# A four-layer graph kernel on one core: the opening's row blocks pass in three groups (0, 1-3, 4-7) instead of two halves

## The chip, the core and the metric

One NeuronCore of a Trainium2 chip. The metric is device time in microseconds (us) of one execution; lower is better. Matrices are float32.

## The reference, cut to what matters

x is 4096 x 128, adj is 4096 x 4096 (about one entry in a thousand, and the diagonal, are not zero). Four graph layers follow one another, each on h = relu(layernorm(x)), each added to x. Only the first touches the change:

```python
h = jnp.maximum(_layernorm(x, axis=-1), 0.0)
x = x + _L0_gnn_ref(L0_gnn_t, h, adj, L0_gnn_alpha, L0_gnn_W, L0_gnn_b)

def _L0_gnn_ref(t, x, A, alpha, W, b):
    a = alpha[0]
    A_prime = a * A
    diag = jnp.diagonal(A_prime) + (1.0 - a)
    A_prime = A_prime.at[jnp.arange(N), jnp.arange(N)].set(diag)
    out_degree = A_prime.sum(axis=1)
    inv_deg = jnp.where(out_degree == 0.0, 0.0, 1.0 / out_degree)
    x = inv_deg[:, None] * A_prime @ x
    x = x @ W.T + b
    return jax.nn.relu(x)
```

The later layers are two-head graph attention (1), one-head graph attention (2), both masked by adj > 0, and a product with adj turned, divided by column sums (3).

## The kernel before, in words

The 4096 rows are 32 row blocks of 128 (T = 32), in four quarters of S = 8 blocks. X keeps all row blocks in on-chip memory, G keeps for each row block what the product with the adjacency reads: here relu(layernorm(x)) times the turned weight W0, which the code calls projected. Stage 0 computes acc = adj x G, one quarter of the result rows at a time: `run(0, q, hooks)` on TensorE goes over k = 0 to 31, and for each k multiplies the adjacency tile k (128 x 1024, 512 KB, from in_adj_t) with G's row block k: eight products of 128 x 129 columns, L488, each of which appears in the trace as two records. A hook is a step that TensorE runs after a certain k. SyncE (SP) issues the loads of x and of the tiles in one order on one queue; eight slots hold tiles, so tile k + 8 is issued when TensorE has read tile k (slot_used) and VectorE has masked it (mask_made, L1361, which writes adj > 0 as bytes for the later layers).

Before k = 0 the row blocks 0 to 7 must be normalised and projected. This opening does it thus. SP loads blocks 0-3 (256 KB, x_first), 4-7 (256 KB, x_loaded[0]), then W0 (64 KB, w0_loaded), adjacency tiles 0 and 1, blocks 8-15, tiles 2 to 7, blocks 16-23. TensorE runs seven warm-up products (L628, WARM = 7), turns the eight blocks (L633) into two banks of PSUM, one for each half, waits for ScalarE's copy of each half to U (L819), multiplies with a centring matrix (identity less 1/128, L638), which subtracts the mean, waits for ScalarE's relu of each half into V (L822), and projects each half by W0 (L645). VectorE meanwhile takes the statistics of the eight blocks (L1127, L1131), combines them to the variance (L1134 to L1140), and after ScalarE's square root (L800) takes the reciprocal (L1146). ScalarE scales blocks 0-3 into G (L830), VectorE blocks 4-7 (L1347). In the same program order VectorE then begins its masks, one for each tile, and between them, after masks 0, 1 and 2, does the statistics of blocks 8-15 and their scale and shift (L1127 to L1150). ScalarE normalises these (L788) into V, and TensorE turns them (L519) in the hook of k = 5, and projects them (L542) in the hook of k = 6; blocks 16-23 follow in the hooks of k = 12 and 14, blocks 24-31 in those of 18 and 21. run(0, 0) waits for G's row block k at each k below 5, and at k = 8, 16 and 24.

Each engine executes its instructions in program order, and waits are on semaphores: an engine that waits holds up all that stands behind on it.

Of the kernel before, what the change touches and what calls it, by code (L numbers as in the profile page):

```python
# [30 lines left out]
P = 128  # L31
ALU = mybir.AluOpType
# [4 lines left out]
EPS = 1e-5  # L37
# [27 lines left out]
def graph_layers(nc, x, adj, adj_t, diag, alpha, w0_t, bias0, ff0, ff0_t, ff1_t, attn, g1, b1, g2, b2,  # L65
                 w2, w2_t, a2, out, inputs1):
    N, D = x.shape
# [19 lines left out]
    WARM = 7  # L87

    with ExitStack() as ctx:
# [73 lines left out]
        one = mix[:, 2, 0:P]  # L163
        U2 = U[:, 0:QC].rearrange("p (c i) -> p c i", c=2)
# [173 lines left out]
        def _(sp):  # L338
# [42 lines left out]
            load_x(0, S // 2, x_first)  # L381
            load_x(S // 2, S // 2, x_loaded[0])
# [96 lines left out]
        def _(pe):  # L479
# [147 lines left out]
            for i in range(WARM):  # L627
                pe.matmul(one, V[:, 0, :], V[:, 0, :], start=True, stop=True, skip_group_check=True)  # L628
            pe.wait_ge(consts_made, 2)
            for half in range(2):  # L630
                pe.wait_ge(x_loaded[0] if half else x_first, 16)
                for s in range(half * HALF, (half + 1) * HALF):
                    mm = pe.transpose(turn[:, s * P:(s + 1) * P], X[:, s, :], ident[:, :])  # L633
                mm.then_inc(f_turned if half else h_turned, 1)
            pe.wait_ge(centre_made, 1)
            for half in range(2):
                pe.wait_ge(xt_kept, half + 1)
                pe.matmul(turn[:, half * BANK:(half + 1) * BANK], centre, U[:, half * BANK:(half + 1) * BANK],  # L638
                          start=True, stop=True, skip_group_check=True).then_inc(x_centred, 1)
            pe.wait_ge(w0_loaded, 16)  # L640
            own = [feed(0, p, w0T, D, 0, 0) for p in range(Q)]
            for half in range(2):
                pe.wait_ge(f_wide if half else h_wide, 1)
                for s in range(half * HALF, (half + 1) * HALF):
                    mm = pe.matmul(mixed[:, s * P:(s + 1) * P], V[:, s, :], w0T, start=True, stop=True, skip_group_check=True)  # L645
                mm.then_inc(f_projected if half else h_projected, 1)
# [8 lines left out]
            run(0, 0, {5: own[1][0], 6: own[1][1], 12: own[2][0], 14: own[2][1], 18: own[3][0], 21: own[3][1],  # L655
# [121 lines left out]
        def _(act):  # L777
# [37 lines left out]
            def first_rows():  # L815

                for half in range(2):
                    act.wait_ge(f_turned if half else h_turned, 1)
                    act.copy(U[:, half * BANK:(half + 1) * BANK], turn[:, half * BANK:(half + 1) * BANK]).then_inc(xt_kept, 1)  # L819
                for half in range(2):  # L820
                    act.wait_ge(x_centred, half + 1)
                    act.activation(V[:, half * HALF:(half + 1) * HALF, :], turn[:, half * BANK:(half + 1) * BANK]  # L822
                                   .rearrange("p (s d) -> p s d", d=D), ACT.Relu).then_inc(f_wide if half else h_wide, 1)
                    if half == 0:
                        deviation(f_var, 1, f_dev)
                act.wait_ge(h_projected, 1)
                act.wait_ge(f_scale, 1)
                settle()
                for s in range(HALF):
                    act.activation(G[:, 0, s, 0:D], mixed3[:, s, :], ACT.Copy, scale=scale[:, s:s + 1])\  # L830
                        .then_inc(h_placed if s < HALF - 1 else f_norm, 1)

            def feed(h, p, q, between=()):
# [17 lines left out]
                else:  # L851
                    deviation(f_var, p - Q + 1 if h > 2 else p + 1, f_dev)
                    act.wait_ge(f_scale, p - Q + 1 if h > 2 else p + 1)
# [259 lines left out]
        def _(dve):  # L1113
# [8 lines left out]

            def statistics(src, made):

                def half():
                    for s in range(S // 2):
                        dve.bn_stats(stats[:, s, :], src(s))  # L1127

                def rest():
                    for s in range(S // 2, S):  # L1130
                        ins = dve.bn_stats(stats[:, s, :], src(s))  # L1131
                    st.then(ins)

                    dve.tensor_tensor(twice, stats[:, :, 1], stats[:, :, 4], ALU.add)  # L1134
                    dve.tensor_tensor(apart, stats[:, :, 1], stats[:, :, 4], ALU.subtract)
                    st.then(dve.tensor_tensor(squares, stats[:, :, 2], stats[:, :, 5], ALU.add))
                    dve.tensor_scalar(mean[:, :], twice, 0.5, None, ALU.mult)
                    dve.tensor_tensor(apart, apart, apart, ALU.mult)
                    st.then(dve.tensor_scalar(squares, squares, 1.0 / D, EPS, ALU.mult, ALU.add))
                    dve.scalar_tensor_tensor(var[:, :], apart, 0.25, squares, ALU.mult, ALU.add).then_inc(made, 1)  # L1140
                return [half, rest]
# [14 lines left out]
            def feed(h, p, q):  # L1156

                c = p - Q + 1 if h > 2 else p + 1
# [172 lines left out]
            dve.memset(V[:, 0, :], 0.0).then_inc(nothing_made, 1)  # L1331
# [4 lines left out]
            own = [feed(0, p, p) for p in range(Q)]  # L1336
# [3 lines left out]
            own[0][0]()  # L1340
            dve.wait_ge(x_loaded[0], 16)
            own[0][1]()
            own[0][2]()

            dve.wait_ge(f_scale, 1)
# [343 lines left out]
```

## Time and profile before

| | us |
|---|---|
| median of three runs | 1197.39 |
| lowest, highest | 1197.26, 1198.12 |
| span of the profiled execution | 1195.6 |
| PE (TensorE matmul) busy | 1190.9 |
| DVE (VectorE) busy | 939.5 |
| ACT (ScalarE) busy | 301.6 |

The span runs from the first to the last instruction of one profiled execution; the runs' times hold what lies around it too. A timeline row gives the start, the time from there to the end of the last of its instructions, the engine, line, operation, what is written from what, their count, and in brackets the idle time of the engine before it and what ended that. Matmul records overlap: the step from one start to the next is shorter than the duration of one.

### The profile page before, as it was taken

How to read it: one execution, taken by the hardware profiler on the slowest of the kernel's cores; microseconds unless marked ns; L12 is line 12 of the kernel's file. 1: busy time of each engine (PE TensorE's matmuls, PEld its weight loads, DVE VectorE, ACT ScalarE, POOL GpSimd, SP SyncE). 2: the span in 40 equal slices, each digit the busy share in tenths (PEclk: the TensorE clock that was granted, in tenths of full speed). 3: DMA queues.
4: the chain of work that ended last, by engine and by line, in shares of the span. 5: the costliest groups of instructions: out<-in, count | busy, mean ns of one | idle time of the engine just before them, and what ended most of it. 6: DMA issues, size and time to landing. Idle time of an engine off the chain costs nothing.

```text
span 1195.6 us, 16808 instructions
## 1 busy us (share of the span) xinstructions
PE 1190.9 (100%) x6299; PEld 823.9 (69%) x6299; DVE 939.5 (79%) x1704; ACT 301.6 (25%) x732; POOL 10.0 (1%) x21
## 2 busy tenths in 40 slices
PE   9999999999999999999999999999999999999999
PEld 9999999965444444444554547999999974444455
DVE  5448675798978787889788797798787869886886
ACT  3312122235323242422333144541212121000000
POOL 3000000000000000000000000000000000000000
PEclk9999999999999999999999999999999999999999
DMA  9888888700111102110000000022303068999830
GB/s 324 295 269 293 295 292 302 254 25 8 46 18 36 18 35 35 53 18 18 1 18 0 18 1 19 2 90 106 141 0 141 1 261 305 310 334 319 320 86 18
DMA packets 79284, 153.18 MB, mean 128 GB/s; under 512 B 35456, under 2 KB 44016, under 8 KB 79216
## 3 DMA queue, kind: packets, MB, share of 16 engines
q1 hardware_dynamic: 53264, 145.43, 34.8%
q10 hardware_dynamic: 25456, 6.30, 2.4%
q8 instruction: 43, 0.70, 0.2%
q0 software_dynamic: 496, 0.55, 0.2%
q14 instruction: 25, 0.20, 0.1%
HBM read 144.33 MB, written 4.24 MB: 124 GB/s over the span
## 4 chain that ended last, share of the span: by engine, by line
PE 98%; DVE 1%; ACT 0%; issue 0%; DVEq 0%
PE acc L504 51%; PE acc L488 37%; PE acc L761 4%; PE mix L570 1%; PE mix L557 1%; PE mix L542 1%; PE turn L519 1%; PE acc L769 1%; DVE ring L1323 0%; PE turn L515 0%; PE mix L628 0%; ACT V L788 0%; DVE U L1454 0%; PE turn L638 0%; PE mix L645 0%
## 5 line engine op out<-in xcount | busy, mean ns | idle before, releaser
L1323 DVE SCALAR_TENSOR_TENSOR ring<-G,score,mask 128x1024 f32<-128x1024 f32 x372 | 467.0, 1280 | 76.5 <-PE acc L504 42.9
L504 PE MATMUL acc<-ring,G 128*128 128x512 f32 x1000 | 436.2, 593 | 0.2 <-DVE acc L1263 0.2
L504 PEld LDWEIGHTS acc<-ring,G 128*128 128x128 f32 x1000 | 186.7, 190 | 227.0 <-issue 213.4
L488 PE MATMUL acc<-G,ring 128*128 128x129 f32 x2240 | 253.8, 275 | 0.0
L488 PEld LDWEIGHTS acc<-G,ring 128*128 128x128 f32 x2240 | 252.0, 192 | 0.8 <-issue 0.8
L488 PE MATMUL acc<-G,mask 128*128 128x129 f32 x1648 | 186.2, 275 | 0.0
L488 PEld LDWEIGHTS acc<-G,mask 128*128 128x128 f32 x1648 | 185.0, 192 | 0.0
L504 PE MATMUL acc<-mask,G 128*128 128x512 f32 x384 | 165.8, 593 | 0.0
L1597 DVE TENSOR_TENSOR ring<-ring,mask 128x1024 f32<-128x1024 f32 x120 | 146.8, 1223 | 10.7
L504 PEld LDWEIGHTS acc<-mask,G 128*128 128x128 f32 x384 | 72.6, 190 | 90.9 <-issue 89.7
L1361 DVE TENSOR_SCALAR mask<-mask 128x1024 uint8<-128x1024 f32 x103 | 68.5, 689 | 38.0 <-DMA mask<-in_adj_t 37.6
L800 ACT ACTIVATE dev<-var 128x8 f32<-128x8 f32 x28 | 5.9, 209 | 230.9 <-DVE var L1140 230.9
L978 ACT COPY U<-acc 128x512 f32<-128x512 f32 x22 | 12.9, 586 | 171.6 <-PE acc L504 171.6
L761 PE MATMUL acc<-mask,G 128*128 128x384 f32 (+1 forms) x128 | 48.6, 540 | 0.0
L986 ACT COPY U<-acc 128x387 f32<-128x387 f32 (+1 forms) x24 | 10.4, 446 | 129.7 <-PE acc L488 128.9
L761 PEld LDWEIGHTS acc<-mask,G 128*128 128x128 f32 x128 | 24.2, 190 | 24.0 <-issue 15.6
L788 ACT ACTIVATE V<-X,shift,scale 128x128 f32<-128x128 f32 (+1 forms) x88 | 35.0, 481 | 0.0
L784 ACT ACT_TABLE_LOAD x26 | 33.4, 1283 | 2.7 <-ACT V L788 1.6
L780 ACT COPY cols<-ident 128x1 f32<-128x1 f32 x40 | 7.6, 190 | 83.0 <-DVE V L1177 23.4
L788 ACT ACTIVATE V<-U,shift,scale 128x128 f32<-128x128 f32 x64 | 25.5, 481 | 6.4 <-DVE shift L1150 6.4
L1177 DVE SCALAR_TENSOR_TENSOR V<-G,ring 128x128 f32<-128x128 f32 x96 | 21.3, 288 | 5.3 <-ACT G L788 5.2
L788 ACT ACTIVATE U<-U,inv 128x128 f32<-128x128 f32 x64 | 19.5, 388 | 0.0
(210 smaller groups left out, 692.9 us busy)
## 6 DMA issues: line engine op xcount, KB each, us to landing
mask<-in_adj SPq DMA_DIRECT2D x128, 512.0 KB, 5.5
mask<-in_adj_t SPq DMA_DIRECT2D x103, 512.0 KB, 4.9
ring<-in_adj_t SPq DMA_DIRECT2D x18, 512.0 KB, 5.0
G<-given_rows SPq DMA_DIRECT2D x10, 512.0 KB, 3.9
G<-in_adj_t SPq DMA_DIRECT2D x4, 512.0 KB, 5.3
inputs<-V ACTq DMA_DIRECT2D x4, 512.0 KB, 2.7
V<-inputs SPq DMA_DIRECT2D x4, 512.0 KB, 3.9
X<-in_x SPq DMA_DIRECT2D x3, 512.0 KB, 8.6
```

The costliest lines, as they stand in the source:

```text
L488: mm = pe.matmul(acc[:, b, (s % 3) * DW:(s % 3) * DW + DW], lhs[:, s * P:(s + 1) * P], g, start=(k == 0 and s % 3 == 0), stop=(k == T - 1) ...
L504: mm = pe.matmul(acc[:, c, :], g, moving[:, c * BANK:(c + 1) * BANK], start=(k == 0), stop=(k == T - 1), skip_group_check=True)
L519: mm = pe.transpose(turn[:, s * P:(s + 1) * P], V[:, s, :], ident[:, :])
L542: mm = pe.matmul(dst, U[:, s * P:(s + 1) * P], weights, start=True, stop=True, skip_group_check=True)
L761: mm = pe.matmul(acc[:, c, 0:n], G[:, 0, k, 0:P], stream3[:, k, c * BANK:c * BANK + n], start=(k == 0), stop=(k == T - 1), skip_group_chec ...
L784: act.activation(warm[func], ident[:, 0:1], func)
L788: ins = act.activation(dst(s), src(s), func, bias=add(s), scale=mul(s))
L978: act.copy(U2[:, c, :], acc2[:, c, :]).then_inc(acc_taken, 1)
L1177: ins = dve.scalar_tensor_tensor(V[:, s, :], blocks(G[:, 1, :, :], q, 1, s)[:, 0, 0:D], 1.0, dot_w[c], ALU.mult, ALU.mult, accum_out=block ...
L1323: dve.scalar_tensor_tensor(slots[k % L], late_home[h] if early and k >= EARLY else rows_home[h, q], rank[h][:, k:k + 1], span(mask, (q * T ...
L1361: dve.tensor_scalar(span(mask, (q * T + k) * QC, QC), tile0(q, k), 0.0, None, ALU.is_gt).then_inc(mask_made, 1)
L1597: dve.tensor_tensor(added, stream3[:, 0, :] if k == 1 else added, stream3[:, k, :], ALU.add).then_inc(tile_added, 1)
```

## The change

The eight row blocks of the opening go in three groups of one, three and four blocks. Block 0 is loaded alone (64 KB), blocks 1-7 in one load (448 KB). Group 0 is turned and centred in bank 0 of `turn` and projected into `one` (bank 2 of `mix`), group 1 in bank 1 of `turn` and in bank 0 of `mix`, group 2 in bank 0 of `turn` again and in bank 1 of `mix`. TensorE's warm-ups become four ahead and two single ones between steps, into bank 2 of `acc`. On TensorE the order is: turn 0, centre 0, turn 1, wait for W0, project 0, turn 2, centre 1, project 1, then k = 0, centre 2, k = 1, project 2, k = 2. VectorE takes block 0's statistics and scale by themselves, then those of blocks 1-7; after that it waits, as before, for the projection of blocks 4-7 and scales them into G, ahead of its first mask. ScalarE copies, rectifies, takes two square roots and scales in the order of the groups. The counts that later steps wait for on f_var and f_scale are one higher.

```diff
--- before.py
+++ after.py
@@ -84,7 +84,8 @@
     EB = len(EDGE)
     SPARE = 2
     WEIGHTS = 15
-    WARM = 7
+    WARM = 4
+    STARTS = (slice(0, 1), slice(1, S // 2), slice(S // 2, S))
 
     with ExitStack() as ctx:
         def sb(name, shape, dt=F32):
@@ -161,6 +162,8 @@
         mixed = mix[:, 0:2, :].rearrange("p b c -> p (b c)")
         mixed3 = mixed.rearrange("p (s d) -> p s d", d=D)
         one = mix[:, 2, 0:P]
+        turned_x = (turn[:, 0:P], turn[:, BANK:BANK + (HALF - 1) * P], turn[:, 0:HALF * P])
+        projected_x = [one if s == 0 else mixed[:, s * P:(s + 1) * P] for s in range(S)]
         U2 = U[:, 0:QC].rearrange("p (c i) -> p c i", c=2)
         acc2 = acc[:, 0:2, :]
 
@@ -378,8 +381,8 @@
                         sp.wait_ge(tile_added, (q - 1) * (T - 1) + max(k, 1))
                     sp.dma_start(stream3[:, k, :], span(adj[k * P:(k + 1) * P, :], q * QC, QC)).then_inc(deep_loaded[k], 16)
 
-            load_x(0, S // 2, x_first)
-            load_x(S // 2, S // 2, x_loaded[0])
+            load_x(0, 1, x_first)
+            load_x(1, S - 1, x_loaded[0])
             sp.dma_start(w0T, w0_t).then_inc(w0_loaded, 16)
             layer0(0, range(2))
             load_x(S, S, x_loaded[1])
@@ -624,26 +627,40 @@
 
 
             pe.wait_ge(nothing_made, 1)
-            for i in range(WARM):
-                pe.matmul(one, V[:, 0, :], V[:, 0, :], start=True, stop=True, skip_group_check=True)
+            def warm_up(n):
+                for i in range(n):
+                    pe.matmul(acc[:, NB - 1, 0:P], V[:, S - 1, :], V[:, S - 1, :], start=True, stop=True, skip_group_check=True)
+
+            def turn_x(g):
+                pe.wait_ge(x_loaded[0] if g else x_first, 16)
+                for i, s in enumerate(range(S)[STARTS[g]]):
+                    mm = pe.transpose(turned_x[g][:, i * P:(i + 1) * P], X[:, s, :], ident[:, :])
+                mm.then_inc(h_turned if g < 2 else f_turned, 1)
+
+            def centre_x(g):
+                pe.wait_ge(xt_kept, g + 1)
+                some = slice(STARTS[g].start * P, STARTS[g].stop * P)
+                pe.matmul(turned_x[g], centre, U[:, some], start=True, stop=True, skip_group_check=True).then_inc(x_centred, 1)
+
+            def project_x(g):
+                pe.wait_ge(h_wide if g < 2 else f_wide, g + 1 if g < 2 else 1)
+                for s in range(S)[STARTS[g]]:
+                    mm = pe.matmul(projected_x[s], V[:, s, :], w0T, start=True, stop=True, skip_group_check=True)
+                mm.then_inc(h_projected if g < 2 else f_projected, 1)
+            warm_up(WARM)
             pe.wait_ge(consts_made, 2)
-            for half in range(2):
-                pe.wait_ge(x_loaded[0] if half else x_first, 16)
-                for s in range(half * HALF, (half + 1) * HALF):
-                    mm = pe.transpose(turn[:, s * P:(s + 1) * P], X[:, s, :], ident[:, :])
-                mm.then_inc(f_turned if half else h_turned, 1)
+            turn_x(0)
+            warm_up(1)
             pe.wait_ge(centre_made, 1)
-            for half in range(2):
-                pe.wait_ge(xt_kept, half + 1)
-                pe.matmul(turn[:, half * BANK:(half + 1) * BANK], centre, U[:, half * BANK:(half + 1) * BANK],
-                          start=True, stop=True, skip_group_check=True).then_inc(x_centred, 1)
+            centre_x(0)
+            turn_x(1)
             pe.wait_ge(w0_loaded, 16)
+            project_x(0)
+            turn_x(2)
+            centre_x(1)
+            warm_up(1)
+            project_x(1)
             own = [feed(0, p, w0T, D, 0, 0) for p in range(Q)]
-            for half in range(2):
-                pe.wait_ge(f_wide if half else h_wide, 1)
-                for s in range(half * HALF, (half + 1) * HALF):
-                    mm = pe.matmul(mixed[:, s * P:(s + 1) * P], V[:, s, :], w0T, start=True, stop=True, skip_group_check=True)
-                mm.then_inc(f_projected if half else h_projected, 1)
 
             def scores_behind_projections():
                 pe.wait_ge(weights_loaded, 16 * WEIGHTS)
@@ -652,7 +669,7 @@
                     mm = pe.matmul(one[:, 2 * h:2 * h + 2], raw, attnc[:, 2 * h:2 * h + 2], start=True, stop=True,
                                    skip_group_check=True)
                 mm.then_inc(qv_summed, 1)
-            run(0, 0, {5: own[1][0], 6: own[1][1], 12: own[2][0], 14: own[2][1], 18: own[3][0], 21: own[3][1],
+            run(0, 0, {0: lambda: centre_x(2), 1: lambda: project_x(2), 5: own[1][0], 6: own[1][1], 12: own[2][0], 14: own[2][1], 18: own[3][0], 21: own[3][1],
                        28: scores_behind_projections})
 
             def turn_weights_back():
@@ -814,21 +831,37 @@
 
             def first_rows():
 
-                for half in range(2):
-                    act.wait_ge(f_turned if half else h_turned, 1)
-                    act.copy(U[:, half * BANK:(half + 1) * BANK], turn[:, half * BANK:(half + 1) * BANK]).then_inc(xt_kept, 1)
-                for half in range(2):
-                    act.wait_ge(x_centred, half + 1)
-                    act.activation(V[:, half * HALF:(half + 1) * HALF, :], turn[:, half * BANK:(half + 1) * BANK]
-                                   .rearrange("p (s d) -> p s d", d=D), ACT.Relu).then_inc(f_wide if half else h_wide, 1)
-                    if half == 0:
-                        deviation(f_var, 1, f_dev)
-                act.wait_ge(h_projected, 1)
-                act.wait_ge(f_scale, 1)
-                settle()
-                for s in range(HALF):
-                    act.activation(G[:, 0, s, 0:D], mixed3[:, s, :], ACT.Copy, scale=scale[:, s:s + 1])\
-                        .then_inc(h_placed if s < HALF - 1 else f_norm, 1)
+                def columns(g):
+                    return slice(STARTS[g].start * P, STARTS[g].stop * P)
+
+                def keep_turned_x(g):
+                    act.wait_ge(h_turned if g < 2 else f_turned, g + 1 if g < 2 else 1)
+                    act.copy(U[:, columns(g)], turned_x[g]).then_inc(xt_kept, 1)
+
+                def keep_centred_x(g):
+                    act.wait_ge(x_centred, g + 1)
+                    act.activation(V[:, STARTS[g], :], turned_x[g].rearrange("p (s d) -> p s d", d=D), ACT.Relu)\
+                        .then_inc(h_wide if g < 2 else f_wide, 1)
+
+                def place(g):
+                    act.wait_ge(h_projected, g + 1)
+                    act.wait_ge(f_scale, 2 if g else 1)
+                    settle()
+                    for s in range(S)[STARTS[g]]:
+                        act.activation(G[:, 0, s, 0:D], projected_x[s], ACT.Copy, scale=scale[:, s:s + 1])\
+                            .then_inc(h_placed if s < HALF - 1 else f_norm, 1)
+                keep_turned_x(0)
+                keep_centred_x(0)
+                act.wait_ge(f_var, 1)
+                act.activation(dev[:, 0:1], var[:, 0:1], ACT.Sqrt).then_inc(f_dev, 1)
+                keep_turned_x(1)
+                place(0)
+                keep_centred_x(1)
+                act.wait_ge(f_var, 2)
+                act.activation(dev[:, 1:], var[:, 1:], ACT.Sqrt).then_inc(f_dev, 1)
+                keep_turned_x(2)
+                place(1)
+                keep_centred_x(2)
 
             def feed(h, p, q, between=()):
 
@@ -849,8 +882,8 @@
                     first_rows()
                     return
                 else:
-                    deviation(f_var, p - Q + 1 if h > 2 else p + 1, f_dev)
-                    act.wait_ge(f_scale, p - Q + 1 if h > 2 else p + 1)
+                    deviation(f_var, p - Q + 2 if h > 2 else p + 2, f_dev)
+                    act.wait_ge(f_scale, p - Q + 2 if h > 2 else p + 2)
                     settle()
                     if h == 4:
                         normalise(lambda s: blocks(G[:, 0, :, :], q, 1, s)[:, 0, 0:D], of_x, local(scale), local(shift),
@@ -1120,6 +1153,18 @@
             def wide(t):
                 return t[:, :].unsqueeze(2).broadcast_to([P, S, D])
 
+            def moments(made, some=slice(0, S)):
+
+                def of(t):
+                    return t[:, some]
+                dve.tensor_tensor(of(twice), stats[:, some, 1], stats[:, some, 4], ALU.add)
+                dve.tensor_tensor(of(apart), stats[:, some, 1], stats[:, some, 4], ALU.subtract)
+                st.then(dve.tensor_tensor(of(squares), stats[:, some, 2], stats[:, some, 5], ALU.add))
+                dve.tensor_scalar(of(mean), of(twice), 0.5, None, ALU.mult)
+                dve.tensor_tensor(of(apart), of(apart), of(apart), ALU.mult)
+                st.then(dve.tensor_scalar(of(squares), of(squares), 1.0 / D, EPS, ALU.mult, ALU.add))
+                dve.scalar_tensor_tensor(of(var), of(apart), 0.25, of(squares), ALU.mult, ALU.add).then_inc(made, 1)
+
             def statistics(src, made):
 
                 def half():
@@ -1130,14 +1175,7 @@
                     for s in range(S // 2, S):
                         ins = dve.bn_stats(stats[:, s, :], src(s))
                     st.then(ins)
-
-                    dve.tensor_tensor(twice, stats[:, :, 1], stats[:, :, 4], ALU.add)
-                    dve.tensor_tensor(apart, stats[:, :, 1], stats[:, :, 4], ALU.subtract)
-                    st.then(dve.tensor_tensor(squares, stats[:, :, 2], stats[:, :, 5], ALU.add))
-                    dve.tensor_scalar(mean[:, :], twice, 0.5, None, ALU.mult)
-                    dve.tensor_tensor(apart, apart, apart, ALU.mult)
-                    st.then(dve.tensor_scalar(squares, squares, 1.0 / D, EPS, ALU.mult, ALU.add))
-                    dve.scalar_tensor_tensor(var[:, :], apart, 0.25, squares, ALU.mult, ALU.add).then_inc(made, 1)
+                    moments(made)
                 return [half, rest]
 
             def scales(got, n, done, keep=None):
@@ -1155,7 +1193,7 @@
 
             def feed(h, p, q):
 
-                c = p - Q + 1 if h > 2 else p + 1
+                c = p - Q + 2 if h > 2 else p + 2
 
                 def first_scales():
                     wait(dve, f_norm, p)
@@ -1328,21 +1366,28 @@
             def diagonal(q, s):
                 return span(mask, q * ((T + S) * QC) + s * (QC + P), P)
 
-            dve.memset(V[:, 0, :], 0.0).then_inc(nothing_made, 1)
+            dve.memset(V[:, S - 1, :], 0.0).then_inc(nothing_made, 1)
             for i in range(2):
                 dve.memset(G[:, i, :, D], 1.0)
             dve.memset(G[:, 1, :, D - 1], 1.0)
             st.mark(dve.memset(hmean, 0.0))
-            own = [feed(0, p, p) for p in range(Q)]
+            own = {p: feed(0, p, p) for p in range(1, Q)}
             dve.wait_ge(consts_made, 2)
             dve.tensor_scalar(centre, ident[:, :], 1.0 / D, None, ALU.subtract).then_inc(centre_made, 1)
             dve.wait_ge(x_first, 16)
-            own[0][0]()
+            st.then(dve.bn_stats(stats[:, 0, :], X[:, 0, :]))
+            moments(f_var, slice(0, 1))
+            dve.wait_ge(f_dev, 1)
+            dve.reciprocal(scale[:, 0:1], dev[:, 0:1]).then_inc(f_scale, 1)
             dve.wait_ge(x_loaded[0], 16)
-            own[0][1]()
-            own[0][2]()
-
-            dve.wait_ge(f_scale, 1)
+            for s in range(1, S):
+                ins = dve.bn_stats(stats[:, s, :], X[:, s, :])
+            st.then(ins)
+            moments(f_var, slice(1, S))
+            dve.wait_ge(f_dev, 2)
+            dve.reciprocal(scale[:, 1:], dev[:, 1:]).then_inc(f_scale, 1)
+
+            dve.wait_ge(f_scale, 2)
             dve.wait_ge(f_projected, 1)
             dve.tensor_tensor(G[:, 0, HALF:S, 0:D], mixed3[:, HALF:, :], scale[:, HALF:].unsqueeze(2).broadcast_to([P, HALF, D]),
                               ALU.mult).then_inc(f_placed, 1)
```

## Rows read from the trace of the kernel before

**Rows 1.** The page: busy time and share by engine; shares of the chain by engine.
```profile
PE 1190.9 (100%) x6299; PEld 823.9 (69%) x6299; DVE 939.5 (79%) x1704; ACT 301.6 (25%) x732; POOL 10.0 (1%) x21
...
PE 98%; DVE 1%; ACT 0%; issue 0%; DVEq 0%
```

**Rows 2.** Timeline of PE, 0 to 30 us.
```profile
1.07 3.35 PE L628 MATMUL mix<-V 128*128 128x128 f32 x14 [1.07 <-DVE V L1331]
4.21 1.63 PE L633 MATMUL turn<-ident,X 128*128 128x128 f32 x8
6.04 1.96 PE L638 MATMUL turn<-U,ring 128*128 128x512 f32 x4 [0.20 <-ACT U L819]
7.92 2.02 PE L645 MATMUL mix<-ring,V 128*128 128x128 f32 x16
9.78 10.88 PE L488 MATMUL acc<-G,mask 128*128 128x129 f32 x96
20.50 1.04 PE L519 MATMUL turn<-ident,V 128*128 128x128 f32 x8
21.37 1.95 PE L488 MATMUL acc<-G,mask 128*128 128x129 f32 x16
```

**Rows 3.** Waits of PE, 0 to 280 us: us in total, times, longest.
```profile
PE turn L638 <- ACT U L819: 0.2, 1, 0.2
```

**Rows 4.** Timeline of PE, narrow: the transposes that start by 5.3 us.
```profile
4.21 1.41 PE L633 MATMUL turn<-ident,X 128*128 128x128 f32 x6
```

**Rows 5.** Timeline of ACT, 0 to 26 us.
```profile
5.31 1.15 ACT L819 COPY U<-turn 128x512 f32<-128x512 f32 x2 [3.07 <-PE turn L633]
7.17 0.60 ACT L822 ACTIVATE V<-turn 128x512 f32<-128x512 f32 x1 [0.71 <-PE turn L638]
...
9.18 1.14 ACT L830 ACTIVATE G<-mix,scale 128x128 f32<-128x128 f32 x4
...
15.46 3.18 ACT L788 ACTIVATE V<-X,shift,scale 128x128 f32<-128x128 f32 x8
21.57 1.07 ACT L812 COPY U<-turn 128x512 f32<-128x512 f32 x2 [2.92 <-PE turn L519]
```

**Rows 6.** Timeline of DVE, 0 to 25 us.
```profile
3.79 0.87 DVE L1127 BATCH_NORM_STATS2 stats<-X 128x6 f32<-128x128 f32 x4 [2.05 <-DMA X<-in_x]
4.62 0.87 DVE L1131 BATCH_NORM_STATS2 stats<-X 128x6 f32<-128x128 f32 x4
...
6.25 0.17 DVE L1140 SCALAR_TENSOR_TENSOR var<-parts 128x8 f32<-128x8 f32 x1
...
10.05 0.69 DVE L1347 TENSOR_TENSOR G<-mix,scale 128x512 f32<-128x512 f32 x1 [1.75 <-PE mix L645]
...
15.17 0.17 DVE L1150 SCALAR_TENSOR_TENSOR shift<-mean,scale 128x8 f32<-128x8 f32 x1
...
24.67 0.69 DVE L1361 TENSOR_SCALAR mask<-mask 128x1024 uint8<-128x1024 f32 x1 [3.36 <-DMA mask<-in_adj_t]
```

**Rows 7.** SP's issues, W0 and tiles 0, 1, 2: start; then KB, us to landing.
```profile
1.80 0.51 SPq L383 DMA_DIRECT2D ring<-in_w_t  x1
2.36 0.91 SPq L365 DMA_DIRECT2D mask<-in_adj_t  x2
...
3.79 4.58 SPq L365 DMA_DIRECT2D mask<-in_adj_t  x6
...
ring<-in_w_t SPq DMA_DIRECT2D x1, 64.0 KB, 4.1
mask<-in_adj_t SPq DMA_DIRECT2D x1, 512.0 KB, 4.8
mask<-in_adj_t SPq DMA_DIRECT2D x1, 512.0 KB, 6.9
mask<-in_adj_t SPq DMA_DIRECT2D x1, 512.0 KB, 8.6
```

**Rows 8.** Groups of ACT by shape, 0 to 60 us: busy us, mean ns.
```profile
L882 ACT COPY G<-mix 128x384 f32<-128x384 f32 x6 | 2.6, 484 | 12.9 <-PE mix L542 12.9
```

## Prediction: what the three groups do to the time

> **What bounds the kernel now.** I read the page's busy shares and its chain of waits first: TensorE (PE) is busy 100% of the span and the chain that ends last is 98% PE [rows 1]. So the time is the sum of what PE executes plus what it waits, and the list of PE's waits is the next view: over the opening and all of stage 0 it holds, after PE's start, one wait of 0.2 us [rows 3]. Anything that makes PE wait once is therefore paid in full, and nothing later takes it back. Then PE's timeline of the opening: warm-ups from 1.07, transposes from 4.21, centring from 6.04, projections from 7.92, the adjacency run from 9.78, without a hole in it until 20.50, where the transposes of row blocks 8 to 15 (hook of k = 5) stand [rows 2]. In it the reader is to see that the opening is already nearly dense: 8 + 4 + 16 records of real work fill 4.21 to 9.78.
>
> The step of one record is the key to all sums. The run: 96 records in 10.88 us, the last lasting 0.275, so 0.1116 us each, and 16 of them, 1.79 us, for one adjacency tile. Projections: 16 records in 2.02, nearly the same. A 512-column record steps 0.43, a first one 0.5 (four in 1.96, the last lasting 0.59) [rows 2]. The warm-ups and first transposes step 0.213, twice as much (six transposes in 1.41, the sixth lasting 0.345) [rows 2, 4]: TensorE is at 1.2 GHz there and at 2.4 GHz from about 5.4 on, after it had been busy without a pause since 1.07. (The clock column shows no drop there; the steps do.)
>
> Then the vector and scalar engines' timelines, for who feeds the hook of k = 5. The vector engine (DVE) is in order: it scales blocks 4 to 7 into G at 10.05 (L1347, as soon as the last projection at 9.67 is out), only then masks tile 0 and takes the statistics of blocks 8 to 15, so that their shift ends at 15.34 [rows 6]. The scalar engine (ACT) normalises them from 15.46 to 18.64 [rows 5]. PE could turn them from about 18.64 + 0.14 = 18.78; it does at 20.50. **That is a slack of 1.7 us**, and no view of waits shows it, since nobody waits.
>
> **The change, part by part.** I lay PE's new order on the time axis of this execution. Lags, from the rows: a transpose's start to ACT's start 0.46 slow (4.86 to 5.31; the first half's last transpose is the fourth of the slow steps from 4.21), 0.31 fast; end of ACT to PE's start 0.14 (5.90 to 6.04; 7.77 to 7.92) [rows 2, 4, 5]. ACT on 512 columns takes 0.59, on 384 columns 0.48, on 128 about 0.36 [rows 5, 8].
> Warm-ups: seven become four, eight records, over at 2.94. Block 0 alone: a 64 KB load is not in the trace. It ends between 2.9 (no use before PE is free) and 3.77, when the 256 KB did [rows 6]; I take 3.1, nearer the low end as it is a quarter of the bytes on an idle queue. It hardly matters, as w0 gates behind it. Transpose of block 0 at 3.2; ACT copy 3.66 to 4.02; centring of 128 columns at 4.16, two slow records; relu 4.85 to 5.21. Group 1's three transposes at 4.7 (blocks 4 to 7 land at 4.6 now [rows 6], and the bytes ahead are the same), 5.13 the last, copy 5.58 to 6.06.
> Projection of block 0 waits for w0, issued at 1.80 and landed 4.1 later, 5.9 [rows 7]. Before, this wait stood behind both centrings and cost nothing; now it stands ahead of group 2's transposes. Start at 6.05; two records to 6.27; four transposes to 6.71; centring of 384 columns (0.32 a record) at 6.71 to 7.36, its end out at 7.53; relu 7.57 to 8.05 (ACT has placed block 0 in between); one warm-up fills in; projection of blocks 1 to 3 at 8.20, six records. **Tile 0's run starts at 8.87, 0.9 earlier than now**. Tile 0 has landed (2.36 + 4.8 = 7.2) [rows 7].
> But centring and projection of group 2 now stand behind k = 0 and k = 1: run k = 0 to 10.66, centring of 512 columns to 11.52, k = 1 to 13.31 (tile 1 landed at 9.7), projection of four blocks, its last record at 14.09, k = 2 at 14.20. Before, k = 2 began at 9.78 + 32 x 0.1116 = 13.35. **So PE is 0.85 later at k = 2**, though the run began earlier: PE's work is the same, less one warm-up that was over before 4.2 anyway, and it now waits some 0.6 us for w0 and some 0.7 for block 1 to 3's round trip over ACT.
> Vector engine: statistics of block 0, then seven blocks (0.193 each from 5.5), variances at about 7.9 where they were at 6.4 [rows 6]. ACT needs them only ahead of group 2's copy (used at 10.7) and the scale only at 9.1: hidden, by 1 us or more. But L1347 waits for the last projection: its release moves from 9.67 to 14.09, 4.43 later, and all behind it on this in-order engine goes along: mask of tile 0, statistics and shift of blocks 8 to 15 (15.34 to 19.77), ACT's eight normalisations (to 23.07). PE reaches the hook of k = 5 at 20.50 + 0.85 = 21.35 and waits until 23.21. **Sum: 4.43 - 1.72 = 2.7 us over now, of which 1.9 is a new wait at the hook.** Behind it the hook's copies and the projection at k = 6 follow PE at the old distances.
> Queues: SP issues tile 8 only when tile 0 is masked; the mask stands right behind L1347, so it moves with it by 4.43 from about 11.4, tiles 9 to 13 by up to 3. The DMA queue is full then: tile 8 came at 24.67 with the vector engine idle [rows 6], so the later issue lies behind transfers still under way. The masks catch up (tiles 3 to 7, 0.69 or less each [rows 6], between 19.7 and 23.2). If that cover were gone, tile 8 could come 2.1 + 2.7 us later before PE missed it. Cost nil. Moving load issues, the new banks and the shifted semaphore counts cost nothing.
>
> A weighing. The trace has TensorE at 2.4 GHz only after an unbroken stretch of work from 1.07 [rows 2, 4]; in the new order PE waits briefly near 3.0, 3.9, 4.6 and 5.4 to 6.0. The Trainium skill (TensorE: Matmul & The Clock Gate, "The HAM clock gate") says that the array runs at half rate until it has seen sustained activity. By it the full clock may be granted later here; the rival below prices that from rows.
>
> **The rivals.**
> 1. The clock comes later. For: the holes just named; against: each is short, the longest some 0.6 us. If PE stays at 1.2 GHz until the projection of blocks 1 to 3: +0.2 on block 0's projection, +0.4 on transposes, +0.6 on centring, so tile 0 starts near 10.05, later than it does now, and the change doesn't even do what it says; the sum is +3.9: 1201.3. Into tile 0: +4.5 and more.
> 2. Only PE's own order counts: the vector chain gets through sooner than I make it (or w0 comes without delay and PE's return is earlier), so that the wait at k = 5 is nearly nothing. Then +0.85 or less, down to +0.2 with w0 at 5.2: 1198.2 down to 1197.6. Against: the vector engine shows no idle gap from 10.05 to 15.34 but is simply in order, so the shift is rigid.
> 3. On the other side: the early start is kept, since group 2's steps find PE waiting for something anyway. Place: k = 2. The price has a floor: tile 2, issued at 3.79, lands 8.6 later, 12.4 [rows 7], against its read at 13.35, so at most 0.9 is gained: 1196.5. It decides if group 2's projection were out by 11.4 (9.67 + 1.7); PE's order puts it behind two tiles of 1.79 and a centring of 0.86 after 8.87, so against.
>
> **How the numbers follow.** The profiled execution's span is 1195.6 and the median of the runs 1197.39, 1.8 more for what lies around the span and between executions; I keep that: span 1198.3, predicted 1197.4 + 2.7 = 1200.1. Own range of this case: w0 at 5.2 instead of 5.9 takes 0.5 off (the copy of group 1 then gates at 6.2), durations of 128-column steps and the clock's edge by some tenths either way: +1.9 to +3.3, 1199.3 to 1200.7. A measurement of this kernel can tell about 0.2%, 2.4 us, so the line lies at 1199.8, inside that range. Chances: forecast 0.60 (0.42 above the line, 0.18 below), clock 0.20, PE's order only 0.12, gain kept 0.06, something unseen that makes it over 2.4 faster 0.02. So slower 0.62, same 0.36, faster 0.02. The range leaves out the gain and the longest half-clock cases: 1197.6 to 1202.0.
>
> **What would show it.** In the changed profile: PE's run L-lines starting near 8.9 (10 or later for rival 1, with 0.213 steps beyond 6 us); L1347's counterpart near 14.2 to 14.3; ACT's normalisation of blocks 8 to 15 near 19.9 to 23.1; transposes of the hook near 23.2 with a new PE wait of 1.9 on ACT (absent for rivals 2 and 3); k = 2 at 14.2; nothing else shifted against PE. I am wrong if the hook's transposes start before 22.5, or if PE waits anywhere later for a tile.

## The result and the profile after

| | before | after |
|---|---|---|
| median, us | 1197.88 | 1201.52 |
| lowest to highest | 1197.26 to 1198.12 | 1200.15 to 1202.07 |
| runs | 7 | 7 |
| span of the profiled execution | 1195.6 | 1200.0 |

The ratio is 1.0031 with a 95% interval of 1.0021 to 1.004: the change makes the kernel 3.6 us slower. The forecast was 2.7 us slower, 1200.1, with a range that reached to 1202.0.

The first view is the list of PE's waits over the whole execution (what waits, for whom, us in total, times, longest). The kernel before had in the opening only the wait of 0.2 us [rows 3]; the kernel after has two new long ones, of 1.6 and 0.7 us (L522's second wait, some 0.4, and the lines left out here stand in the list before too):

```profile
PE turn L522 <- ACT V L805: 2.1, 2, 1.6
PE acc L632 <- DVE V L1369: 1.1, 1, 1.1
PE turn L637 <- DMA X<-in_x: 0.7, 1, 0.7
...
PE mix L648 <- ACT V L843: 0.2, 1, 0.2
```

The timeline of PE, which answers to [rows 2]:

```profile
1.07 2.08 PE L632 MATMUL acc<-V 128*128 128x128 f32 x8 [1.07 <-DVE V L1369]
2.94 0.42 PE L637 MATMUL turn<-ident,X 128*128 128x128 f32 x1
3.15 0.63 PE L632 MATMUL acc<-V 128*128 128x128 f32 x2
3.81 0.77 PE L643 MATMUL turn<-U,ring 128*128 128x128 f32 x2
5.32 0.90 PE L637 MATMUL turn<-ident,X 128*128 128x128 f32 x3 [0.75 <-DMA X<-in_x]
6.01 0.63 PE L648 MATMUL mix<-ring,V 128*128 128x128 f32 x2
6.44 1.06 PE L637 MATMUL turn<-ident,X 128*128 128x128 f32 x4
7.29 1.49 PE L643 MATMUL turn<-U,ring 128*128 128x384 f32 x2
8.57 0.63 PE L632 MATMUL acc<-V 128*128 128x128 f32 x2
9.36 1.29 PE L648 MATMUL mix<-ring,V 128*128 128x128 f32 x6 [0.15 <-ACT V L843]
10.48 1.95 PE L491 MATMUL acc<-G,mask 128*128 128x129 f32 x16
12.27 1.02 PE L643 MATMUL turn<-U,ring 128*128 128x512 f32 x2
13.13 1.95 PE L491 MATMUL acc<-G,mask 128*128 128x129 f32 x16
14.91 1.06 PE L648 MATMUL mix<-ring,V 128*128 128x128 f32 x8
15.81 7.31 PE L491 MATMUL acc<-G,mask 128*128 128x129 f32 x64
24.74 1.09 PE L522 MATMUL turn<-ident,V 128*128 128x128 f32 x8 [1.62 <-ACT V L805]
```

Tile 0 starts at 10.48 (9.78 before), k = 2 at 15.81 (13.35 before, 2.46 later), and in the hook of k = 5 PE waits 1.62 us, so that the transposes stand at 24.74 instead of 20.50, 4.24 later. That execution took 1201.75, and the spans differ by 4.4 us, so nearly all of it has arisen by this line. The steps tell TensorE's clock (the profile's clock column reads 1.00 throughout): the four transposes from 6.44 step 0.213 and the two 384-column records last 1.49 from 7.29, half rate, 1.2 GHz; from k = 0 on 16 records take 1.95, steps of 0.112, the full 2.4 GHz. The step changes within the projection of blocks 1 to 3, near 10.1, against 5.4 before.

Who keeps PE at the hook: the timelines of DVE and ACT, which answer to [rows 6] and [rows 5].

```profile
9.44 0.20 DVE L1388 RECIPROCAL scale<-dev 128x7 f32<-128x7 f32 x1 [1.77 <-ACT dev L861]
16.09 0.69 DVE L1392 TENSOR_TENSOR G<-mix,scale 128x512 f32<-128x512 f32 x1 [6.45 <-PE mix L648]
16.69 0.68 DVE L1406 TENSOR_SCALAR mask<-mask 128x1024 uint8<-128x1024 f32 x1
...
21.21 0.17 DVE L1188 SCALAR_TENSOR_TENSOR shift<-mean,scale 128x8 f32<-128x8 f32 x1
...
25.50 0.69 DVE L1406 TENSOR_SCALAR mask<-mask 128x1024 uint8<-128x1024 f32 x1 [1.11 <-DMA mask<-in_adj_t]
```
```profile
21.51 3.18 ACT L805 ACTIVATE V<-X,shift,scale 128x128 f32<-128x128 f32 x8
```

The reader is to see one number go through: the placing of blocks 4 to 7 moves from 10.05 to 16.09, 6.04 later, and the shift of blocks 8 to 15 from 15.17 to 21.21 and ACT's normalisations from 15.46 to 21.51 go with it, by 6.04 and 6.05. DVE stands idle for 6.45 us ahead of the placing. Blocks 8 to 15, whose statistics come behind it, are issued at 3.24 and land 7.6 us later, at 10.8; from then on, for some 5 us, only its own order keeps DVE from them.

And the loads. SP issues block 0 at 0.8 and blocks 1 to 7 at 1.2; KB and us to landing of each:

```profile
X<-in_x SPq DMA_DIRECT2D x1, 64.0 KB, 2.0
X<-in_x SPq DMA_DIRECT2D x1, 448.0 KB, 4.1
```

Busy times by stretch, of which only the last two columns matter here (share of the DMA engines, GB/s); first after, then before:

```profile
2.40:3.20 0.80, 0.80 (x6) 0.79 (x6) 0.39 (x3) 0.00 (x0) 0.00 (x0) 1.00 0.38 40
3.20:4.00 0.80, 0.78 (x4) 0.52 (x4) 0.65 (x7) 0.27 (x1) 0.00 (x0) 1.00 1.10 329
```
```profile
2.40:3.20 0.80, 0.80 (x6) 0.80 (x6) 0.00 (x0) 0.00 (x0) 0.00 (x0) 1.00 1.04 312
```

Block 0 lands at 2.8, blocks 1 to 7 at 1.2 + 4.1 = 5.3, where blocks 4 to 7 had landed at 4.6 [rows 6]. From 2.4 to 3.2 us the queue moves 40 GB/s where it had moved 312: block 0's 64 KB are nearly through by 2.4, and little of the next load flows until 3.2.

### The profile page after: what moved, and what is told of

Same layout as the page of the kernel before. It is cut to its first block, busy times and chain, and to the rows that moved or that the text cites. A ratio compares the mean times of both kernels' runs of the same rounds, so it can differ in the third digit from the quotient of the medians.

```text
span 1200.0 us, 16820 instructions
## 1 busy us (share of the span) xinstructions
PE 1192.9 (99%) x6299; PEld 824.8 (69%) x6299; DVE 940.2 (78%) x1711; ACT 302.1 (25%) x736; POOL 9.6 (1%) x21
## 3 DMA queue, kind: packets, MB, share of 16 engines
HBM read 144.33 MB, written 4.24 MB: 124 GB/s over the span
## 4 chain that ended last, share of the span: by engine, by line
PE 97%; DVE 1%; ACT 1%; DMA 0%; issue 0%; SPq 0%; DVEq 0%
PE acc L507 50%; PE acc L491 36%; PE acc L778 4%; PE mix L573 1%; PE mix L560 1%; PE mix L545 1%; PE turn L522 1%; PE acc L786 1%; ACT V L805 1%; DMA X<-in_x 0%; DVE ring L1361 0%; PE turn L518 0%; PE mix L648 0%; PE turn L643 0%; DVE U L1499 0%
```

## The experiments

All times are set against the kernel before, run between them on the same chip; the table gives the medians, the ratio of all times with its 95% interval (not the quotient of the two medians: where the times fall into groups it is another), and from the profile when k = 2 and the hook's transposes start.

| kernel | median, us | before, us | ratio | k = 2 | hook |
|---|---|---|---|---|---|
| before | 1197.88 | | | 13.35 | 20.50 |
| after | 1201.52 | 1197.88 | 1.0031 (1.0021 to 1.004) | 15.81 | 24.74 |
| after, again | 1201.9 | 1197.47 | 1.0036 (1.0022 to 1.0049) | 16.02 | 24.99 |
| statistics early | 1199.59 | 1197.58 | 1.0016 (1.0007 to 1.0025) | 15.29 | 22.44 |
| pause filled | 1200.31 | 1197.58 | 1.0024 (1.0015 to 1.0034) | 14.52 | 23.45 |
| both | 1198.61 | 1197.58 | 1.001 (1.0001 to 1.0019) | 14.46 | 21.61 |
| group 2 ahead | 1200.38 | 1197.58 | 1.0023 (1.0014 to 1.0032) | 16.28 | 23.43 |
| statistics early, loads in halves | 1198.67 | 1197.59 | 1.0008 (0.9999 to 1.0017) | 14.54 | 21.69 |
| both, three loads | 1198.69 | 1197.59 | 1.0008 (0.9998 to 1.0017) | 14.52 | 21.67 |
| before, no warm-ups | 1198.18 | 1197.59 | 1.0004 (0.9995 to 1.0014) | 13.58 | 20.73 |
| before, block 0 alone | 1199.64 | 1197.59 | 1.0013 (1.0004 to 1.0022) | 14.15 | 21.30 |
| before, six warm-ups | 1197.33 | 1197.47 | 0.9999 (0.999 to 1.0008) | 13.26 | 20.41 |

(Where k = 2 is within a run of records without a hole, its start is that run's start and 32 steps of 0.1116. The start is PE's order alone; the hook has the waits for the other engines too.)

**Theory H**: PE pays in full a wait in the hook of k = 5, which the vector engine's order makes. **Rival C**: the later clock is the whole loss. The kernel after, the two edits by themselves and both together are the four corners of that question; "group 2 ahead" is one more way to undo the cause.

Statistics early (on the kernel after):

```diff
             dve.wait_ge(f_scale, 2)
+            dve.wait_ge(x_loaded[1], 16)
+            own[1][0]()
+            own[1][1]()
             dve.wait_ge(f_projected, 1)
...
+            dve.wait_ge(f_placed, 1)
+            own[1][2]()
...
-            masks(0, at([0, 1, 2, 8, 9, 11, 16, 17, 19], own_feed(1) + own_feed(2) + own_feed(3)))
+            masks(0, at([8, 9, 11, 16, 17, 19], own_feed(2) + own_feed(3)))
```

> VectorE takes the statistics of blocks 8-15 while it idles before the placing of blocks 4-7 instead of between its first masks. Theory H (the wait in the hook of k = 5 is paid in full): TensorE's wait of 1.62 us there goes, the hook's transposes start right behind k = 5 (15.81 + 7.15 = 22.96 instead of 24.74), so the time is about 1.8 us below the changed kernel and 2.4 above the kernel before. Rival C (the late clock is the whole loss): the wait comes back at another place and the time is that of the changed kernel, +3.6 to +4.2.

Measured 1.0016, against 1.0031 and 1.0036 of the kernel after: 1.8 to 2.4 us come back, and +2.0 over the kernel before is left. DVE does the statistics as soon as blocks 8 to 15 have landed:

```profile
11.22 0.87 DVE L1172 BATCH_NORM_STATS2 stats<-X 128x6 f32<-128x128 f32 x4 [1.75 <-DMA X<-in_x]
```

The timeline of PE in the stretch of the hook has no wait in brackets any more:

```profile
15.29 7.31 PE L491 MATMUL acc<-G,mask 128*128 128x129 f32 x64
22.44 1.04 PE L522 MATMUL turn<-ident,V 128*128 128x128 f32 x8
```

H holds; C falls as the whole cause. In this execution the clock came at 8.4, not at 10.1, hence k = 2 at 15.29 instead of 15.81; so not all that came back is the hook's. The clean price comes further on, from two kernels with the clock at the same moment.

Pause filled (on the kernel after):

```diff
             centre_x(0)
+            warm_up(3)
             turn_x(1)
```

> Three more warm-up products (six records of 0.213 us, 1.28 in all) stand where TensorE waits for blocks 1-7, from 4.24 to 5.3. If the pause is what holds back the full clock, the records step 0.11 from about 5.5 to 7 on instead of from 10.1, some 2.5 us of slow work take half the time, and with 0.2 lost to the longer fill the time is 1.0 to 1.2 us below the changed kernel; the hook's wait stays at 1.5 to 1.7. Rival: the pause has no part in it; the clock comes near 10 again and the time is the changed kernel's or 0.2 above.

The steps fall to 0.11 at 6.1 us, k = 2 starts at 14.52, 1.29 before that of the kernel after, and the hook still waits 1.6 us, since the placing and PE moved together:

```profile
23.45 1.09 PE L522 MATMUL turn<-ident,V 128*128 128x128 f32 x8 [1.62 <-ACT V L806]
```

The time is 1.0024, 0.8 to 1.4 us below the kernel after by the two ratios of it: as expected for the clock's part. All ten times lie below 1201.2, where ten of the kernel after's twelve lie above 1201.45, so the earlier clock is not that of one profiled execution alone.

> Both edits. If the hook's wait and the late clock are two separate terms they add: 1.8 + 1.1 = 2.9 us below the changed kernel, +1.2 to +1.4 over the kernel before. If one hides behind the other, the time is that of the better of the two.

1.001: 2.5 to 3.1 us below the kernel after, where 2.9 was expected. The two terms add. Against "pause filled", whose clock came at 6.1 where it came at 6.0 here, the early statistics give back 1.7 us (1200.31 to 1198.61): that is the hook's price with the clock held still. What is left, +1.0 (0.1 to 2.3 by the interval), is the change without a wait at the hook and without a late clock, and its timeline shows where it lies:

```profile
5.64 0.66 PE L637 MATMUL turn<-ident,X 128*128 128x128 f32 x3
...
8.37 0.94 PE L648 MATMUL mix<-ring,V 128*128 128x128 f32 x6 [0.36 <-ACT V L844]
9.14 1.95 PE L491 MATMUL acc<-G,mask 128*128 128x129 f32 x16
```

PE turns group 1 at 5.64 and starts k = 0 at 9.14, 0.64 before the kernel before did; but with group 2's centring and projection still to come it is 1.1 later at k = 2 (14.46 against 13.35).

Group 2 ahead (on the kernel after):

```diff
             project_x(1)
+            centre_x(2)
+            project_x(2)
...
-            run(0, 0, {0: lambda: centre_x(2), 1: lambda: project_x(2), 5: own[1][0], ...
+            run(0, 0, {5: own[1][0], ...
```

> Centring and projection of blocks 4-7 stand ahead of k = 0 again, all else as changed. TensorE now waits about 0.9 us for ScalarE's relu of group 2 (no tile to run meanwhile), so k = 0 starts near 13.1; but VectorE's placing moves from 16.1 to about 13.3 and the hook's wait goes. Theory H: 0.9 below the changed kernel, +3.3 over the kernel before, no wait at the hook. Rival (the interleaving with k = 0 and k = 1 is a gain of its own and the hook's wait costs nothing): 0.9 above the changed kernel.

1.0023, 1.0 to 1.6 us below the kernel after, more than the expected 0.9, part of it in the profiled execution again an earlier clock (8.4). A new wait of 0.69 us stands ahead of group 2's projection, where no tile covers ACT's relu; the placing is at 12.99 and the hook's wait is gone:

```profile
11.72 1.16 PE L648 MATMUL mix<-ring,V 128*128 128x128 f32 x8 [0.69 <-ACT V L845]
12.71 10.88 PE L491 MATMUL acc<-G,mask 128*128 128x129 f32 x96
23.43 1.04 PE L522 MATMUL turn<-ident,V 128*128 128x128 f32 x8
```

So interleaving group 2 with k = 0 and 1 does save PE that 0.69, and pays for it with 1.6 at the hook.

**The loads.** What does the load of block 0 alone do? Two kernels with the statistics early ask it: one takes the old loads back and has its three further warm-ups at the start (`WARM = 7`), the other splits the loads finer and has one further warm-up in the pause. A third asks it of the kernel before.

> The three groups with the statistics of blocks 8-15 early (as in e1), but the loads as before the change (blocks 0-3, then 4-7) and seven warm-ups, so that TensorE is busy from 1.07 on. If the single-block load is what delays blocks 1-7 (5.2 instead of 4.6) it lands blocks 0-3 by 3.8 and 4-7 by 4.6, the clock comes near 5.4 to 6, k = 0 starts near 8.9 and k = 2 near 14.2: +0.8 over the kernel before, 0.2 below e3. Rival (blocks 1-7 came late by chance): the same as e3, +1.0 to +1.2.

Blocks 4 to 7 land at 4.6 again, and the clock comes at 5.3; but W0 landed at 6.25 in this execution and PE waited 0.3 us for it; k = 0 starts at 9.22. The ratio, 1.0008, can't be told from the 1.001 of "both". The gain of 0.2 that I expected is not shown.

> e3 with blocks 0, 1-3 and 4-7 as three loads (64, 192, 256 KB) and a wait of its own for each, one warm-up product in place of the three of the fill. If the queue pauses after a small first load (the second load's data start only near 3.2 whatever its size), blocks 4-7 still land near 5.2, and blocks 1-3 near 4.1; TensorE turns group 1 from 4.8 instead of 5.65 and k = 0 starts up to 0.5 earlier, unless W0 (5.4) holds the projection of block 0: then 0.2 earlier. If the size of the 448 KB load is the reason, blocks 4-7 land near 4.6.

Issues of the three loads, KB and us to landing:

```profile
X<-in_x SPq DMA_DIRECT2D x1, 256.0 KB, 3.3
X<-in_x SPq DMA_DIRECT2D x1, 192.0 KB, 2.6
X<-in_x SPq DMA_DIRECT2D x1, 64.0 KB, 1.9
```

Blocks 1 to 3, issued at 1.2, land at 3.8, and 4 to 7, issued at 1.7, at 5.0: 0.4 later than before the change, 0.3 sooner than in the kernel after. I had expected 4.1 and 5.2 if a small first load holds up the queue, and 4.6 for blocks 4 to 7 if the 448 KB were the reason. 0.4 of the 0.7 us remains without a load of that size, so it is not the whole reason; how the rest divides is not shown. The time is that of "both".

Block 0 alone on the kernel before (only the two loads, and all transposes and statistics wait for both):

> The kernel before with the new loads alone: block 0 by itself, 1-7 in one load, all transposes and statistics wait for both. If the small first load costs the second its start, blocks 1-7 land near 5.2 instead of 4.6 and TensorE's transposes start near 5.3 instead of 4.2: a new wait of about 0.9, and +1.0 to +1.1 in the time, more if the clock comes later too. If the late landing in the changed kernel was chance: transposes at 4.7, +0.5.

```profile
5.45 1.06 PE L634 MATMUL turn<-ident,X 128*128 128x128 f32 x8 [1.02 <-DMA X<-in_x]
```

A wait of 1.02 us, where 0.9 was expected: the late landing comes with the loads alone. The median is 2.05 us above the kernel before, against an expected 1.0 to 1.1, for the eleven times fall into two groups: 1198.08 to 1198.31 (four) and 1199.55 to 1199.91 (seven), 1.5 apart, some 0.6 and 2.1 us over the kernel before. In the profiled execution, of the first group (1198.29), the full clock came within PE's pause: the eight transposes step 0.11 from 5.6 on. That the second group is that of the late clock is likely by the size, but no profile of it was taken.

No warm-ups in the kernel before (`WARM = 0`):

> The kernel before without its seven warm-up products: nothing else is left out. TensorE starts with the transposes near 3.9 instead of 4.2. If unbroken work from early on brings the full clock at 5.4, it now comes at 7 or later: centrings and projections then step twice as long until there, +0.8 to +1.8. If the warm-ups have no part in it, the clock comes at 5.4 as before and the time falls by 0.3.

```profile
3.75 2.01 PE L633 MATMUL turn<-ident,X 128*128 128x128 f32 x8 [3.75 <-DMA X<-in_x]
5.61 2.63 PE L638 MATMUL turn<-U,ring 128*128 128x512 f32 x4
8.15 2.02 PE L645 MATMUL mix<-ring,V 128*128 128x128 f32 x16
```

+0.5 to +0.6 us, which can't be told from none: below the +0.8 to +1.8 of the one case and above the -0.3 of the other. The centring takes 2.63 instead of 1.96 [rows 2], and its first two records have all of the difference (1.77 where they had 1.96 less two steps of 0.43, 1.10, before):

```profile
5.61 1.77 PE L638 MATMUL turn<-U,ring 128*128 128x512 f32 x2
```

Work at half rate takes twice as long, so 0.67 us more means half rate for some 1.3 us from 5.61: the full clock came near 7.0, some 1.5 us later than in the kernel before, as I had put it ("7 or later"). That was 3.2 us after PE's first record. The time rose less than expected, since PE also started at 3.75 instead of 4.21: k = 0 starts at 10.01, 0.23 later than before.

Six warm-ups (`WARM = 6`), the one kernel that was meant to beat the one before:

> The kernel before with six warm-up products instead of seven. They end at 3.79 instead of 4.21, about when blocks 0-3 land (3.6 to 3.8), so the transposes start near 3.9 with no pause worth the name. If only TensorE's order counts, k = 0 and all behind it come 0.3 earlier: -0.3 against the kernel before, less than can be told surely. Rival: the transposes' slow steps grow by as much as the start gains (the clock comes at a time that does not move with the work): -0.1 or nothing.

The transposes start at 3.84 instead of 4.21, and k = 0 at 9.69 instead of 9.78: of 0.37 some 0.28 are lost again to slow steps, since the clock came at 6.2 here. The times do not differ (0.9999, 0.999 to 1.0008). No version found beats the kernel before.

> The changed kernel again, unaltered, for a second execution with a profile and ten more times. If the moment of the full clock varies from execution to execution, the times spread over 1.5 to 2 us with a few near 1200.2 (clock before 7) and most near 1201.5 (clock at 8.4 to 10.1). If it is fixed at 10.1 by the order of the work, all lie within 0.6 around 1201.5.

The clock came at 10.5 in its profile, k = 2 started at 16.02, the hook's wait was 1.7. The five times lie between 1201.56 and 1202.0: by themselves they look like the fixed moment. But 1200.15 in the first series, 1198.03 with the statistics early (the other ten 1199.23 or more) and 1199.18 and 1199.33 with group 2 ahead (the other nine 1200.31 or more) lie 1 to 1.5 below the rest, as the two groups of "before, block 0 alone" lie apart. So the moment may vary from execution to execution, with the late one the more frequent; no profile of an early one of the kernel after was taken.

## Why the prediction was right, point by point

- **Sign and mechanism: right, and shown.** The slack of 1.7 us that no view of waits shows, the placing that goes along with project 2, the new wait on ACT in the hook of k = 5: it is there with 1.62 (predicted 1.9), and goes by two different edits. Its price, with the clock held still, is 1.7 us.
- **PE's order: right in kind, 1.6 too small.** Predicted +0.85 at k = 2, measured +2.46 in the profile (k = 2 at 15.81 instead of the 14.20 of the sum). The term that was mis-sized is the clock, which the sum let come at 5.4; it came at 10.1. At the projection of block 0 PE was still on the forecast's time (6.01, forecast 6.05). All of the 1.6 arises behind it: group 2's transposes, the 384-column centring and the projection of blocks 1 to 3 at half rate bring k = 0 to 10.48 instead of 8.87. Filling the pause brought k = 2 back by 1.29, to 14.52, though the fill itself let group 1 start 0.3 later (5.64 instead of 5.32).
- **The landing of blocks 1 to 7: wrong.** I kept it at 4.6 "since the bytes ahead are the same"; it was 5.3, and PE waited 0.7 for it. By itself that cost PE's order nothing, since the forecast had put a wait for W0 up to the same moment. Its harm is the pause that it makes, since filling that pause brought the clock forward to 6.1.
- **Rival 1 (the clock comes later) came on top of the forecast.** I had given it 0.20 as an alternative, at +3.9, a price that holds the forecast's +2.7 too. The sign that I had named for it, a start of tile 0 at 10 or later with steps of 0.213 beyond 6 us, is what the profile shows. The measured +3.6, and +4.4 in the second series, lie nearer to it than to the forecast, and 1201.5 is above my own narrow range (1199.3 to 1200.7). It is inside the wide one because that one was drawn to take in most of rival 1, not because the sum was complete. Against it I had said that each pause was short, the longest 0.6: with the later landing one was 0.75.
- **Rival 2 (only PE's order, +0.85 or less): fell.** The hook's wait is there. With it and the late clock both gone +1.0 is left, which is about the size that PE's order had in the sum.
- **Rival 3 (early start kept): fell.** Even with the hook's wait and the late clock both gone k = 2 is 1.1 late.
- **W0: the wait was foreseen and did not come.** W0 landed at 5.5 here (forecast 5.9), before group 1's transposes were out, so the landing of blocks 1 to 7 hid it; in the kernel with loads in halves it landed at 6.25 and cost 0.3.
- **Block 0's landing:** 2.8, taken as 3.1, of no weight. ("A 64 KB load is not in the trace" overlooked W0's [rows 7], though that one stood behind 512 KB.)
- **ACT and DVE durations, lags:** the 384-column copy took 0.48 as taken; the 128-column one 0.27 instead of 0.36; the hook followed ACT by 0.05 (24.69 to 24.74), not 0.14, so the slack was 1.8, not 1.7.
- **Tile issues: cost nil, as said.** Tile 8 was issued at 17.46 and masked at 25.50, 0.83 later than before [rows 6]; PE has no wait for a tile in its list.
- **The skill's rule.** The Trainium skill (TensorE: Matmul & The Clock Gate, "The HAM clock gate") has the array at half rate until it has seen sustained activity; the kernel after, with its pauses, agrees (full clock near 10, near 6 with the largest pause filled). So does the kernel without warm-ups, whose work began later and whose full clock came later (near 7.0), though sooner after its first record (3.2 us) than in any other kernel here.

## What to carry to other kernels

When one engine's order binds, starting its main loop earlier gains nothing if the steps that were ahead of the loop are only moved into it: count the engine's work up to a fixed point behind the move, not up to the loop's start. Then follow each moved step's release through the in-order engines that wait for it, and look for consumers that arrive just after their data: their slack shows in no list of waits and is what a later release uses up first. When an engine is made to wait for a late release, move its independent work ahead of that wait; here that alone gave back 1.7 us, a little under half of the loss.

## What the runs showed of the hardware that I had not expected

A load of 64 KB issued first made the 448 KB behind it land at 5.1 to 5.4 us, in all seven profiled executions with these two loads, instead of 4.6. From 2.4 to 3.2 us the queue moved 40 to 168 GB/s in them, 261 to 312 in the four executions with a first load of 256 KB. With three loads, 64, 192 and 256 KB, it moved 205 there, and the last of the row blocks landed at 5.0.

TensorE's full clock came at very different moments in the profiled executions: 5.3, 5.4, 6.0, 6.1, 6.2 and 7.1 with PE busy nearly without pause, 8.4, 8.4, 10.1 and 10.5 with a pause of about 0.7 us near 5, yet by the end of the pause in one kernel that had idled from 4.4 to 5.5, and near 7.0 in one that began only at 3.8. What decides it is left open; that filling the pause makes it early was seen in both kernels that did so, and in the times of the one that has no other edit.
